# A fourth key product moved ahead of the first scores of a gated cross-attention and channel-mix kernel

## What is computed

```python
x = x + tanh(g_xattn) * attention(layernorm(x), ctx)       # 16 heads, 154 keys, softmax, then @ Wo.T
xn = layernorm(x)
xr = mu_r * xn + (1 - mu_r) * shifted(xn)                   # shifted: the row of the token before
xk = mu_k * xn + (1 - mu_k) * shifted(xn)
r = sigmoid(xr @ W_r.T)
k = square(relu(xk @ W_k.T))
out = x + tanh(g_ffn) * (r * (k @ W_v.T))
```

## Time and profile before

| | us |
|---|---|
| median of 3 runs | 1425.04 (1422.91 to 1425.04) |
| the profiled execution | 1423.38 |
| its span, first to last instruction | 1421.7 |
| PE busy | 1355.7 (95%) |
| DVE busy | 1054.9 (74%) |
| ACT busy | 776.1 (55%) |
| POOL busy | 577.2 (41%) |

### The profile page before, as it was taken

How to read it: one execution, slowest core, us unless ns; L and a number is a source line. 1 busy time by engine, 2 the same in 40 slices (tenths; PEclk the granted TensorE clock), 3 DMA queues, 4 the chain that set the end, 5 groups by cost and what they waited for, 6 DMA issues and landing times.

```text
span 1421.7 us, 27928 instructions
## 1 busy us (share of the span) xinstructions
PE 1355.7 (95%) x9436; PEld 990.4 (70%) x9436; DVE 1054.9 (74%) x1924; ACT 776.1 (55%) x1424; POOL 577.2 (41%) x774
## 2 busy tenths in 40 slices
PE   4989999999999999999999999999999999999988
PEld 3656676776767777676777767677776767777657
DVE  4887778687787868778686877868677786877652
ACT  3583746557374654737466473645637465563632
POOL 2113435344353534435253443525335352534333
PEclk7999999999999999999999999999999999999989
DMA  6631111211012121111212111121201112120101
GB/s 190 219 87 44 40 45 52 73 52 52 22 66 59 52 73 52 47 27 59 66 52 73 38 48 39 59 66 52 66 25 63 44 59 66 52 65 17 45 15 45
DMA packets 98795, 84.07 MB, mean 59 GB/s; under 512 B 49488, under 2 KB 63824, under 8 KB 98768
## 3 DMA queue, kind: packets, MB, share of 16 engines
q1 hardware_dynamic: 98768, 83.72, 19.5%
HBM read 58.79 MB, written 20.71 MB: 56 GB/s over the span
## 4 chain that ended last, share of the span: by engine, by line
PE 75%; DVE 13%; ACT 8%; issue 3%; POOL 1%; DMA 0%; ACTq 0%; DVEq 0%
PE g_bank L1067 41%; PE g_bank L1227 7%; PE o_bank L1174 6%; PE s_bank L1148 4%; PE d_bank L1180 4%; ACT s_bank L638 3%; ACT pq L637 3%; PE s_bank L1124 3%; PE s_bank L1158 2%; DVE buf L780 2%; DVE o_bank L909 2%; ACT buf L543 1%; DVE xa L890 1%; DVE d_bank L909 1%; PE s_bank L1067 1%
## 5 line engine op out<-in xcount | busy, mean ns | idle before, releaser
L850 DVE TENSOR_TENSOR pq<-s_bank,pq 128x512 f16<-128x512 f32 x320 | 220.2, 689 | 69.4 <-ACT s_bank L638 69.1
L846 DVE TENSOR_REDUCE mm<-s_bank 128x3 f32<-128x462 f32 (+1 forms) x384 | 198.8, 577 | 92.9 <-PE s_bank L1124 92.7
L637 ACT ACTIVATE pq<-s_bank 128x512 f16<-128x512 f32 x320 | 192.1, 600 | 86.6 <-PE s_bank L1152 86.6
L1227 PE MATMUL g_bank<-buf,WkT 128*128 128x512 f32 x744 | 196.6, 411 | 12.8 <-DVE buf L780 12.7
L1067 PE MATMUL g_bank<-xnT,WqT 128*128 128x512 f32 x768 | 199.2, 405 | 4.4 <-DVE xnT L834 4.4
L638 ACT ACTIVATE s_bank<-s_bank 128x512 f32<-128x512 f32 x320 | 194.6, 608 | 0.0
L1067 PE MATMUL g_bank<-WoT,buf 128*128 128x512 f32 x768 | 193.3, 401 | 0.0
L1067 PE MATMUL g_bank<-WrT,buf 128*128 128x512 f32 x744 | 184.2, 396 | 0.0
L475 POOL TENSOR_TENSOR buf<-place,buf 128x512 fp32r<-128x512 f32 x64 | 82.6, 1291 | 235.4 <-ACT buf L543 235.4
L1227 PEld LDWEIGHTS g_bank<-buf,WkT 128*128 128x128 f32 x744 | 136.6, 192 | 55.9 <-DVE buf L780 17.5
L1067 PE MATMUL g_bank<-WvT,buf 128*128 128x512 f32 x708 | 174.2, 395 | 0.0
(11 more groups left out here) (140 smaller groups left out, 2096.4 us busy)
## 6 DMA issues: line engine op xcount, KB each, us to landing
xa<-in_x SPq DMA_DIRECT2D x64, 256.0 KB, 3.4
x<-in_x SPq DMA_DIRECT2D x64, 256.0 KB, 2.8
out<-x SPq DMA_DIRECT2D x48, 256.0 KB, 2.0
k_all<-k_scratch SPq DMA_DIRECT2D x16, 256.0 KB, 2.9
k_low<-k_scratch SPq DMA_DIRECT2D x16, 256.0 KB, 3.0
v_main<-v_scratch SPq DMA_DIRECT2D x16, 256.0 KB, 2.8
place<-x SPq DMA_DIRECT2D x16, 256.0 KB, 2.4
out<-place SPq DMA_DIRECT2D x16, 256.0 KB, 2.0
```

What stands on the lines that cost most here:

```text
L637: nc.scalar.activation(pq[:, n, HI, :], bank[:, :], ACT.Exp, scale=SCALE).then_inc(p_hi, 1)
L846: nc.vector.reduce_max(maxima, scores, AX.X).then_inc(reduced, 1)
L850: nc.vector.tensor_tensor(pq[:, n, LO, :], score_bank[5 * g + n][:, :], pq[:, n, HI, :], ALU.subtract).then_inc(p_lo, 1)
L1227: ins = nc.tensor.matmul(bank[c][:, :], WkT2[:, s, e, cols(c)], buf3[:, m, e, :], start=(e, n) == (0, 0), stop=(e, n) == (C - 1, len(PRODU ...
```

## The change

The PE's order of the FFN products in a step with an FFN is changed, and ACT's and DVE's lists follow:

| place on the PE | before | after |
|---|---|---|
| ahead of group 0 | k0 and k1, k2 | k0 and k1, k2, k3 |
| group 0: head / tail | k3 / r0 | r0 / r1 |
| group 1 | r1 / v0 | v0 / r2 |
| group 2 | v1 / r2 | v1 / r3 (last step: v1 / none) |
| group 3 | r3 / v2 (last step: v2 / none) | v2 / none |

The left entry stands between head and tail scores, the right one between tail scores and `values`. The v3 product, and r3 in the last step, stay where they were. On ACT the fourth `xr_high` and the second `k2_high` go ahead of the first exponentials, the third and fourth `k2_high` come between those of group 0, and `tanh_r` is one place earlier. On DVE the relu of k3 moves from behind the fifth `p_low` of group 0 to behind the second, and `gated` of each group to behind its second `p_low`. The banks and the waits of the products are exchanged to match. The diff, cut to its core:

```diff
-        K_BANK = R_BANK = V_BANK = WO_BANK = [g_bank[n] for n in (0, 1, 0, 1)]
+        K_BANK = WO_BANK = [g_bank[n] for n in (0, 1, 0, 1)]
+        R_BANK, V_BANK = [g_bank[n] for n in (0, 1, 1, 1)], [g_bank[n] for n in (0, 0, 0, 1)]
...
                     xr_high(i - 1, 2)
+                    xr_high(i - 1, 3)
+                    k2_high(i - 1, 1)
                 exps(i, 0, 0)
                 exps(i, 0, 1)
                 if ffn:
-                    xr_high(i - 1, 3)
-                    k2_high(i - 1, 1)
+                    k2_high(i - 1, 2)
                 exps(i, 0, 2)
                 exps(i, 0, 3)
+                if ffn:
+                    k2_high(i - 1, 3)
...
                 exps(i, 0, 4)
                 if ffn:
-                    k2_high(i - 1, 2)
                     tanh_r(i - 1, 0)
-                    k2_high(i - 1, 3)
+                    tanh_r(i - 1, 1)
...
-                    if ffn and (pre or g < G - 1):
-                        tanh_r(i - 1, g)
+                    if ffn and (g == 1 or g == 2 and pre):
+                        tanh_r(i - 1, g + 1)
...
                 p_low(i, 0, 1)
+                if ffn:
+                    k_relu(i - 1, 3)
...
                 p_low(i, 0, 4)
-                if ffn:
-                    k_relu(i - 1, 3)
...
-                    if ffn and g == 2:
-                        gated(i - 1, 1, V_BANK[1])
+                    if ffn:
+                        gated(i - 1, g - 1, V_BANK[g - 1])
...
-                    if ffn and g != 2:
-                        gated(i - 1, g - 1, V_BANK[g - 1])
...
                 else:
-                    pe.wait_ge(u_ready, i * TT + t)
+                    pe.wait_ge(th_ready, i * TT + t)
...
-                else:
-                    pe.wait_ge(th_ready, i * TT + t + 1)
+                elif t:
+                    pe.wait_ge(u_ready, i * TT + t + 1)
+                else:
+                    pe.wait_ge(th_ready, i * TT + 1)
...
                     ffn_k(i - 1, (2,), before=at(2, lambda: maxima_transposed(i)))
+                    ffn_k(i - 1, (3,))
...
                 head_scores(i, 0)
                 if ffn:
-                    ffn_k(i - 1, (3,))
+                    ffn_r(i - 1, 0)
...
                 tail_scores(i, 0)
                 if ffn:
-                    ffn_r(i - 1, 0)
+                    ffn_r(i - 1, 1)
...
+                for g in (1, 2):
+                    head_scores(i, g)
+                    if ffn:
+                        ffn_v(i - 1, g - 1)
...
+                    tail_scores(i, g)
+                    if ffn and (g == 1 or pre):
+                        ffn_r(i - 1, g + 1)
...
+                    values(i, g, pre)
 
                 head_scores(i, 3)
-                if ffn and pre:
-                    ffn_r(i - 1, 3)
-                elif ffn:
+                if ffn:
                     ffn_v(i - 1, 2)
...
                 tail_scores(i, 3)
-                if ffn and pre:
-                    ffn_v(i - 1, 2)
```

More of the change, by code:

```diff
@@ L1293, in step @@
                 values(i, 0, pre)
-                head_scores(i, 1)
-                if ffn:
-                    ffn_r(i - 1, 1)
-                else:
[L1299 to L1319, removed]
-                if ffn and pre:
-                    ffn_r(i - 1, 3)
-                elif ffn:
+                for g in (1, 2):
[3 more added lines that the diff above has]
+                    else:
+                        keys_or_values(FIRST_LATER + 2 * g)
+                    tail_scores(i, g)
+                    if ffn and (g == 1 or pre):
+                        ffn_r(i - 1, g + 1)
+                    elif not ffn:
+                        keys_or_values(FIRST_LATER + 2 * g + 1)
+                    values(i, g, pre)
+                head_scores(i, 3)
+                if ffn:
                     ffn_v(i - 1, 2)
```

## The result

The changed kernel takes 1467.26 us (median of four runs, 1466.42 to 1472.31) against 1424.68 for the kernel before: a ratio of 1.0308, 95% interval 1.0287 to 1.0329. It is 3.1% slower. 1474 was forecast, with a range of 1459 to 1484.

A forecast was written before the change was run, and what follows sets the result against it. PE is 95% busy, but each group was taken to last by its ACT and DVE chain against the PE work over it; loop steps 44.1, last step 3.2, clock 3.1: +50.4 us on 1423.4, forecast 1474 us, range 1459 to 1484.

The forecast's parts named there:

- The front: Ahead of group 0's head scores: the fourth k product hides under nothing and delays everything behind it, +2.91 us a step.
- Group 0: Head scores to `values`: last exponential queues behind `k2_high` 3, which waits for POOL's square; +0.58 us a step.
- Group 3: With one product left, the ACT and DVE chain sets its length: 9.50 to 9.16 us, -0.34 a loop step.
- Groups 1 and 2: Middle groups of a loop step keep two products each and have no waits for pq: no cost.
- The step: One loop step: 2.91 + 0.58 - 0.34 = +3.15 us; 14 of them, +44.1 us.
- The last step: Step without transposes, group 2 left with v1 alone: +2.91 + 0.58 - 0.26 = +3.2 us, its clock left as it was.
- The clock: Half clock after group 3's waits in the loop steps: two drops taken, +3.1 us, bounds 0 to 22 us.
- The signs: Expected in the profile: steps of 86.9 us, 12 to 15 more waits for pq, granted clock slightly below 0.989.
- C: Rival: PE the only bound, group 3 shrinks by the whole product to 6.59 us; 1416 us in all; chance 0.03.
- A: Rival: clock drops after group 3 in nearly all 14 loop steps, 1.57 us each; 1493 us; chance 0.10.
- B: Rival: POOL keeps pace, group 0 stays 8.36 us or loses its wait; 1462 or 1455 us; chance 0.15.
- D: Rival: `k2_square` 3 takes 1.5 us or a second filler waits, +0.5 us a step; 1481; 0.15, shared with five to eight drops.

The follow-up runs named there:

- The k product alone: Kernel before with only the fourth k product moved ahead of group 0's head scores and r0 into its place: 1489.52 us, ratio 1.0458; 1472.33 us with the wait filled.
- the late `k2_high`: Changed kernel with the fourth k product's high part on ACT moved behind group 0's fifth exponentials: 1466.12 us, ratio 1.03; 1459.0 us with group 3's waits filled.
- the added product: Changed kernel with an unread second copy of the third v product between tail scores and transposed tiles of group 3: 1473.78 us, ratio 1.0353.
- two matmuls shifted: Kernel before with two matmuls of each group's second product done one group earlier, k3's relu two p_low earlier: 1423.53 us, ratio 0.9999.
- tile inside r3: Kernel before with the same two matmuls shifted, and group 3's first transposed tile moved into r3 ahead of its last chunk: 1424.01 us, ratio 0.9996.

## Why the prediction was right, and what in it was off

**The front: 2.91, measured 2.80.** Half of k2 and k3 are 18 matmuls from 664.70 to 669.07, 4.37 us. In the kernel before half of k2 alone took 647.39 - 645.82 = 1.57 up to its head scores:

```profile
645.82 1.64 PE L1227 MATMUL g_bank<-buf,WkT 128*128 128x512 f32 x6
```

The product is nowhere hidden. The k product alone shows this without the rest of the change.

**Group 0: +0.58, measured +0.55.** The mechanism is the one written down: `k2_high` 3 waits for POOL's square, and the last exponentials stand behind it. It was foreseen 0.55 us late; with the instruction before it started at 674.36 and one every 0.51 us its turn was at 674.87, and it started at 675.41, 0.54 late (the record has 0.44 of idle time). Taking it from there gave 0.57 us back. The wait for `xr_low` 3 was foreseen as 0.5; the last chunk was due at 669.07 + 1.13 + 2.18 = 672.38 and started at 672.84, 0.46 late (0.28 in the record). It was rightly put as one that replaces part of the other; the late `k2_high` shows it as the next in line.

**Group 3: -0.34, measured -0.51.** This is the term of the sum that was mis-sized most. It was read off step 0's group, 9.16 us. ACT in that group, whose head scores start at 91.40:

```profile
91.58 1.52 ACT L582 ACTIVATE xa<-xa,nb,rstd 128x512 f32<-128x512 f32 x2
93.00 0.59 ACT L637 ACTIVATE pq<-s_bank 128x512 f16<-128x512 f32 x1
...
95.74 0.58 ACT L543 ACTIVATE place<-g_bank 128x512 f16<-128x512 f32 x1
96.22 0.59 ACT L543 ACTIVATE xnT<-d_bank 128x512 fp32r<-128x512 f32 x1
```

Two normalizations push the first exponentials to H + 1.60, where a loop step has H + 1.30, and ACT also splits a value product (95.74) ahead of the tile's copy, which a loop step doesn't have. So the copy starts at H + 4.82 there and at H + 4.64 in the loop, before and after (682.72 - 678.08, 704.92 - 700.28). The other reading in the prediction was the better one: p_low 4 over at H + 8.94 in before; it was at 709.22, H + 8.94, again, and the PE went on 0.05 us later, below the 0.1 to 0.24 that was allowed.

**Groups 1 and 2: no cost, measured 7.74 and 7.74** against 7.75 and 7.77. Right. These groups also show that two products without a wait take 7.74 to 7.77 us and not the 7.87 that was worked out as 8.36 - 0.49; so the wait of 0.49 in the record stood for 0.6 us, and in the last step group 2 won 0.16 and not 0.26.

**The step: +3.15, measured +2.81** (86.52 - 83.71). 0.11 of the difference is the front, 0.17 group 3, 0.03 group 0 and 0.04 groups 1 and 2, to within rounding. Over 14 steps that is 4.8 us, and most of the 6.7 us by which 1474 was too high. The last step with what follows it was put at +3.2; it came to 2.95 - 1.95 = +1.0, for a reason that was not foreseen, the clock (below).

**The clock: two falls taken, two in the trace**, at 1.7 us each (447.96 to 451.92 for `values` is 3.96 us, where 709.27 to 711.54 is 2.27). That the count was met is luck: it was a choice between two rows. The same pattern had five falls with the late `k2_high`, and the changed kernel's fourth run, 1472.31 us at a granted clock of 0.986, lost more clock than its other three at 0.989. The last step was left as it was; neither of its two waits of 2.5 us cost clock this time, -1.6 us.

**The signs.** The waits for pq in the list grew by 43 (34 and 30 times, against 19 and 2) and not by 12 to 15; the three in each loop step's group 3 that were named beside that number make 42 by themselves. The mean granted clock was 0.989 both times, and not slightly below.

**The rivals.** C, the PE as the only bound, asked for 6.6 us in group 3; it was 8.99, and the added product shows directly that 2.4 us of the group are free. A, half clock in each loop step, fell for this kernel, and is nearly what happened to the k product alone. B, the small refill, fell with the 0.44 us that ACT waited for POOL, and D's longer one did not come. The Trainium skill's rule on short idles (TensorE: Matmul & The Clock Gate, "A second HAM failure mode: psum-queue depth-cycling"), read as one fall in each step, is not borne out here, with 2 of 14; with waits of 1.20 and 2.09 us in group 0 it was 11 of 14.

## What to carry to other kernels

A busy share of 95% doesn't say that work can be moved freely: between two points of a schedule, time is the longer of the chain and the work laid over it, and a piece that leaves a stretch gives back only what stands above the chain. Read both lengths for each stretch before moving anything, and look for the chain's length in the records of the other engines (where the last p_low ends), not in a similar stretch elsewhere in the program. What remains as a wait on the PE may cost twice, once as time and once through the clock. And a wait in the record is shorter than what it costs the PE, here by 0.1 to 0.3 us; compare starts.

## What the runs showed of the hardware that was not expected

How often the clock falls depends on more than the length of a wait. The same pattern of waits in group 3 (1.02, 0.35 and 0.34 us) was followed by half clock, for 3.4 us, in 2 of 14 steps of 86.5 us, in 5 of 14 steps of 86.0 us (in the trace roughly each third one), and, shortened to 0.68 and 0.34, in none of 14 steps of 85.8 us. Waits of 1.20 and then 2.09 us in group 0 were followed by it in 11 of 14. The last step is the clearest: in the traces of the five kernels in which only group 3 of it has a wait of 2.5 us (before, the two with the k product alone, the two shifted ones) the clock fell each time, between 0.6 us before and 1.2 us after the end of that wait; in the seven in which groups 2 and 3 both have one, it fell at one of the fourteen waits. Why is open: that the step's length decides, or what the PE did ahead of the wait, isn't shown, since the kernels differ in both. Where there are many falls they recur from run to run, as the granted clocks of the k product alone (0.975 to 0.977) and of the late `k2_high` (0.983 to 0.985) show; whether it is none or two a single profile doesn't tell. Matmuls whose results nobody reads, put in the waits, were in five kernels, and none of these lost the clock in a loop step; two of them were faster for it, by 17 and by 7 us, and the changed kernel, with two falls to win back, was not measurably faster.

Up to the first head scores of step 1 the kernel before and the two shifted ones do the same work, and yet these come at 145.2, 148.9 (two matmuls shifted) and 146.8 us (tile inside r3). The nine kernels with the fourth k product in front of them have them between 147.8 and 151.9. In the trace of the first shifted kernel the clock fell at 57 and 88 us. The PE in two stretches, of the shifted kernel and of before:

```profile
57.50:60.50 3.00, 3.00 (x21) 0.50 1.01 339
88.20:91.20 3.00, 3.00 (x10) 0.50 0.00 0
```
```profile
57.50:60.50 3.00, 3.00 (x25) 1.00 1.03 316
88.20:91.20 3.00, 2.08 (x40) 1.00 0.23 87
```

That is some 4 us of scatter between executions which no change of the loop explains, and it goes into the difference of any two spans.
